# Two batches' logit extensions in one run of the tensor engine, with a longer x ring and loads tied to their own stores

## What is computed

```python
base_out = einsum('bti,oi->bto', x, W) + b
y = base_out + (x @ A[slot]) @ Bm[slot] * 2
logits = einsum('bsd,ed->bse', y, route_w)
topk_v, topk_idx = top_k(logits, 1)
route_weight = one_hot(topk_idx) * topk_v
h = einsum('bsd,erd->bser', y, A_ffn)
out = einsum('bser,eor->bso', route_weight[..., None] * h, Bw)
return x + out
```

## Time and profile before

| | |
|---|---|
| median of 3 runs | 289.58 us (289.46 to 289.77) |
| the profiled execution | 289.77 us, of which the span of the trace is 288.0 us |
| busy shares of the span | PE 98%, PEld 79%, DVE 70%, ACT 39%, POOL 4% |
| chain that ended last | PE 98% |
| one whole unit in the steady part | 26.8 us |
| one extension | 3.6 us from its first weight load to the next main product |

### The profile page before, as it was taken

The page is one execution under the profiler, slowest core; times in us unless marked ns, Lnnn a source line. Parts: engine busy times, 40 slices in busy tenths (PEclk is TensorE's granted clock), DMA queues, the critical chain, the costliest instruction groups (busy, mean ns, idle before and its releaser), DMA issues.

```text
span 288.0 us, 4401 instructions
## 1 busy us (share of the span) xinstructions
PE 282.7 (98%) x1700; PEld 226.2 (79%) x1700; DVE 202.4 (70%) x234; ACT 112.6 (39%) x166; POOL 12.5 (4%) x44
## 2 busy tenths in 40 slices
PE   8999999999999999999999999999999999999994
PEld 5999999996766885888588758857885888588993
DVE  0061200077698998799789969896998798699974
ACT  0001300196877532744373355427432642443300
POOL 6300030000000000000000000000000000000000
PEclk9999999999999999999999999999999999999998
DMA  7999999999980247759958993999499769536668
GB/s 250 406 408 395 402 416 411 373 415 424 418 373 6 93 200 272 312 178 404 386 203 296 409 364 137 380 366 381 140 378 391 263 220 420 238 127 256 272 236 277
DMA packets 19591, 88.52 MB, mean 307 GB/s; under 512 B 2410, under 2 KB 5106, under 8 KB 11762
## 3 DMA queue, kind: packets, MB, share of 16 engines
q1 hardware_dynamic: 16128, 84.87, 75.7%
q10 hardware_dynamic: 3442, 3.37, 3.5%
HBM read 54.60 MB, written 33.55 MB: 306 GB/s over the span
## 4 chain that ended last, share of the span: by engine, by line
PE 98%; DVE 0%; DVEq 0%; issue 0%
PE bank_out L661 16%; PE bank_h L738 11%; PE bank_h L739 10%; PE bank_h L740 10%; PE bank_out L699 10%; PE bank_out L701 10%; PE bank_out L700 10%; PE bank_e L723 10%; PE bank_h L668 1%; PE bank_r L661 1%; PE bank_h L661 1%; PE bank_e L661 1%; PE bank_l L675 1%; PE bank_l L661 1%; PE bank_l L749 1%; PE bank_r L758 1%
## 5 line engine op out<-in xcount | busy, mean ns | idle before, releaser
L405 ACT ACTIVATE x_hi<-x_ring 128x1024 fp32r<-128x1024 f32 (+1 forms) x72 | 69.0, 965 | 66.7 <-PE bank_h L740 65.9
L507 DVE TENSOR_TENSOR x_lo<-x_ring,x_hi 128x1024 fp32r<-128x1024 f32 (+1 forms) x72 | 78.9, 1102 | 11.9 <-ACT x_hi L405 10.1
L598 DVE TENSOR_TENSOR x_ring<-bank_out,x_ring 128x1024 f32<-128x1024 f32 (+1 forms) x71 | 78.4, 1106 | 1.7 <-PE bank_out L701 1.2
L738 PE MATMUL bank_h<-x_hi,m_hi 128*128 128x512 f32 (+1 forms) x144 | 54.1, 376 | 0.0
L739 PE MATMUL bank_h<-x_lo,m_hi 128*128 128x512 f32 (+1 forms) x144 | 53.3, 370 | 0.0
L740 PE MATMUL bank_h<-x_hi,m_lo 128*128 128x512 f32 (+1 forms) x144 | 53.2, 369 | 0.0
L699 PE MATMUL bank_out<-wh_hi,bw_hi 128*128 128x512 f32 (+1 forms) x143 | 53.1, 371 | 0.0
L701 PE MATMUL bank_out<-wh_hi,bw_lo 128*128 128x512 f32 (+1 forms) x143 | 53.0, 371 | 0.0
L700 PE MATMUL bank_out<-wh_lo,bw_hi 128*128 128x512 f32 (+1 forms) x143 | 53.0, 371 | 0.0
L661 PE MATMUL bank_out<-pt,w_ring 128*128 128x136 f32 x384 | 46.0, 281 | 0.0
L661 PEld LDWEIGHTS bank_out<-pt,w_ring 128*128 128x128 f32 x384 | 45.4, 192 | 0.7 <-DMA w_ring<-W 0.7
(11 more groups left out here) (79 smaller groups left out, 162.3 us busy)
## 6 DMA issues: line engine op xcount, KB each, us to landing
x_ring<-xT SPq DMA_DIRECT2D x32, 1024.0 KB, 7.6
outT<-x_ring SPq DMA_DIRECT2D x28, 1024.0 KB, 4.8
w_ring<-W SPq DMA_DIRECT2D x30, 512.0 KB, 10.3
outT<-x_ring SPq DMA_DIRECT2D x12, 256.0 KB, 2.9
w_ring<-W SPq DMA_DIRECT2D x4, 256.0 KB, 4.5
x_ring<-loraB ACTq DMA_DIRECT2D x8, 128.0 KB, 10.3
la<-loraA ACTq DMA_DIRECT2D x8, 128.0 KB, 13.1
x_ring<-BwT SPq DMA_DIRECT2D x1, 1024.0 KB, 11.1
```

Source lines behind the costliest of these rows:

```text
L405: act.activation(out, in_, ACT.Copy).then_inc(done, 1)
L507: dve.tensor_tensor(out, a, b, ALU.subtract).then_inc(done, 1)
L598: dve.tensor_tensor(x, out_banks(u, j), x, ALU.add).then_inc(v_out, 1)
L738: mm(h, m_hi[:, c, :], hi, start=(c == 0), stop=False)
```

## The change

Extensions are no longer made one at the head of each batch's unit. At unit 0 comes that of batch 0, at unit 1 those of batches 1 and 2, at unit 3 of 3 and 4, at unit 5 of 5 and 6, at unit 7 that of 7; units 2, 4 and 6 have none at their head. They need two banks, and the second is had by putting the count into the logits' bank. x of the second batch is now read one unit earlier, so the ring has 14 pieces, and the load behind store k is that of piece k + 14, into the slot that this very store empties. Two loads more go out in the first phase. A scratch region is made smaller so that the ring fits.

```diff
-    XRING = 12
+    XRING = 14
...
-        bank_e = psum("bank_e", [P, T])
+        bank_e = [psum(f"bank_e{i}", [P, T]) for i in range(2)]
         bank_h = psum("bank_h", [P, T])
-        bank_r = psum("bank_r", [P, T])
...
+        EXT_RUNS = {0: (0,), 1: (1, 2), 3: (3, 4), 5: (5, 6), 7: (7,)}
...
-            LAG = 2
+            LAG = 0
             LAST = NPIECES - NQ
             for k in range(LAST):
                 store(k)
                 if k >= LAG and k - LAG + XRING < NPIECES:
                     load_x(k - LAG + XRING)
...
-                dve.scalar_tensor_tensor(out=wh[:, :], in0=bank_r[:, :], scalar=0.0, in1=wh[:, :],
+                dve.scalar_tensor_tensor(out=wh[:, :], in0=bank_l[:, :], scalar=0.0, in1=wh[:, :],
...
+            def extension(b):
+                pe.wait_ge(g_ext, b + 1)
+                if b >= 2:
+                    pe.wait_ge(a_top, b - 1)
+                    pe.wait_ge(v_two, b - 1)
+                for r in range(C // NGROUPS):
+                    for g in range(NGROUPS):
+                        c = r * NGROUPS + g
+                        for k in x_pieces(b, c):
+                            if c == 0 or k not in x_pieces(b, c - 1):
+                                x_landed(pe, k)
...
+                        last = mm(bank_e[b % 2][g * GROUP:(g + 1) * GROUP, :], ext[b % 2][:, c, :], x_chunk(b, c),
+                                  start=(r == 0), stop=(r == C // NGROUPS - 1))
+                last.then_inc(t_ext, 1)
...
                 if leads(u):
-                    pe.wait_ge(g_ext, b + 1)
-                    if b >= 1:
-                        pe.wait_ge(a_top, b)
-                        pe.wait_ge(v_two, b)
...
+                    for n in EXT_RUNS.get(b, ()):
+                        extension(n)
...
                         if b >= 1:
-                            pe.wait_ge(a_log, b)
-                            pe.wait_ge(v_ahead, b)
+                            pe.wait_ge(v_w, b)
...
-                        if b >= 1:
-                            pe.wait_ge(v_w, b)
-                        mm(bank_r[:, :], beats[0:JUDGES, :], ahead[0:JUDGES, :], start=True, stop=True).then_inc(t_count, 1)
+                        mm(bank_l[:, :], beats[0:JUDGES, :], ahead[0:JUDGES, :], start=True, stop=True).then_inc(t_count, 1)
...
-    nc = bacc.Bacc("TRN2", target_bir_lowering=False, num_devices=1)
+    nc = bacc.Bacc("TRN2", target_bir_lowering=False, num_devices=1, dynamic_dma_scratch_size=1024)
```

More of the change, by code:

```diff
@@ L101, in adaln_ffn @@
         x_ring = sb("x_ring", [P, XRING, PIECE])
-        lb = x_ring[:, 8, :].rearrange("p (b c r) -> p b c r", b=NB, c=C)
-        bw_raw = x_ring[:, 9, :]
+        lb = x_ring[:, 12, :].rearrange("p (b c r) -> p b c r", b=NB, c=C)
+        bw_raw = x_ring[:, 13, :]
         lb_cols = x_ring[:, 11, :].rearrange("p (c b r) -> p c b r", b=NB, c=C)
-        EARLY = (8, 9, 11)
+        EARLY = (11, 12, 13)
         phase1 = ExitStack()
@@ L242, in w_banks @@
             if blk == 2:
-                return [(bank_e, 4, 1), (bank_h, 5, 1)]
+                return [(bank_e[0], 4, 1), (bank_h, 5, 1)]
             if blk == 3:
-                return [(bank_r, 6, 1), (bank_l, 7, 1)]
+                return [(bank_e[1], 6, 1), (bank_l, 7, 1)]
             return [(bank_out[blk % 2], 2 * blk, 2)]
@@ L438, in _ @@
                     act.wait_ge(t_pb, 1)
-                    copy(pb[:, E:XN], bank_r[0:1, 0:PN], a_bp)
-                    copy(pb[:, 0:E], bank_r[0:1, 0:E], a_bp)
+                    copy(pb[:, E:XN], bank_e[1][0:1, 0:PN], a_bp)
+                    copy(pb[:, 0:E], bank_e[1][0:1, 0:E], a_bp)
                     act.wait_ge(a_bp, 4)
@@ L469, in _ @@
                         act.wait_ge(v_two, b)
-                    act.activation(e_top[:, :], bank_e[2 * GROUP:4 * GROUP, :], ACT.Identity,
+                    act.activation(e_top[:, :], bank_e[b % 2][2 * GROUP:4 * GROUP, :], ACT.Identity,
                                    bias=e_bias[:, 0:1]).then_inc(a_top, 1)
@@ L554, in sum_two @@
                     dve.wait_ge(a_odd, b)
-                dve.tensor_tensor(e_two[:, :], bank_e[0:2 * GROUP, :], e_top[:, :], ALU.add).then_inc(v_two, 1)
+                dve.tensor_tensor(e_two[:, :], bank_e[b % 2][0:2 * GROUP, :], e_top[:, :], ALU.add).then_inc(v_two, 1)
             def sum_all(b):
@@ L680, in _ @@
             pe.wait_ge(g_const, CONSTS)
-            mm(bank_r[:, 0:PN], ones[:, :], pb_sum[(C - 1) % 2][:, :], start=True, stop=True).then_inc(t_pb, 1)
+            mm(bank_e[1][:, 0:PN], ones[:, :], pb_sum[(C - 1) % 2][:, :], start=True, stop=True).then_inc(t_pb, 1)
             for n in range(BP_AT, NWP):
@@ L707, in _ @@
             pe.wait_ge(a_beats, 3)
+            def extension(b):
[9 more added lines that the diff above has]
+                                x_landed(pe, k)
+                        if b == 0 and c % 2 == 0:
+                            pe.wait_ge(a_m, 3 * M_LOTS[c // 2])
+                        last = mm(bank_e[b % 2][g * GROUP:(g + 1) * GROUP, :], ext[b % 2][:, c, :], x_chunk(b, c),
+                                  start=(r == 0), stop=(r == C // NGROUPS - 1))
+                last.then_inc(t_ext, 1)
             for u, (b, t0, nt) in enumerate(UNITS):
                 if leads(u):
-                    pe.wait_ge(g_ext, b + 1)
-                    if b >= 1:
-                        pe.wait_ge(a_top, b)
-                        pe.wait_ge(v_two, b)
[L715 to L725, removed]
+                    for n in EXT_RUNS.get(b, ()):
+                        extension(n)
                 if u >= 1:
```

## The result

The changed kernel takes 323.9 us (median of six runs, 321.4 to 325.7) against 289.6 before (also six runs, 289.5 to 289.8), a ratio of 1.118 with a 95% interval of 1.113 to 1.124. I had said 295.5 and at most 298.8: the sign was right, the size was off by a factor of almost six.

What follows compares the result with a forecast made beforehand. PE, busy without a break in a steady unit, was taken to bound the kernel. The terms -1.0 + 1.7 + 3.3 + 2.0 = +6.0 us on 289.77 gave 295.8, or 295.5 us as median; range 292.0 to 298.8.

Steps and rivals of the forecast that it cites:

- The gain of the switches: Exits from extensions in the second phase: three switches fewer at 0.34 us each, 1.0 us less.
- First and second cost: Heads of units 2, 4, 6: PE waits for `weigh`, 1.7 us in all, and for the first addition, 3.3 us.
- Third cost: SP's queue: each load waits for its store's landing, so loads fall behind and PE waits in units 3 and 5, 2.0 us.
- p: Period of SP's loop per piece while stores are due: taken as 7.1 us, bounds 6.3 and 7.3.
- the harmless value: Period of SP's loop up to which PE loses nothing to late loads: 6.95 us.
- The clock: PE's clock: long gaps may halve it; no size given, only added to the rival of late loads.
- the rival of late loads: Loads much later, full 7.3 us period with second load delayed, or piece 11 late: above 298.5 us; chance 0.07.
- The fixed-cost estimate: SP's loop: 2.0 us plus two 1 MB transfers at 2.4 each, 6.8 us, no wait, 293.7 us whole; not chosen.
- Edits at nothing: Count in the logits' bank, two more first-phase loads, smaller scratch: claimed to cost nothing.

Runs made afterwards that it cites:

- the control: The kernel before, with only DVE's and ACT's order changed (additions moved ahead, chain of sums closed up): 289.4 us, ratio 0.9996.
- `LAG = 1`: The changed kernel with the load behind store k being that of piece k + 13, which waits for the store one piece back: 293.6 us, ratio 1.0125.

## Why the prediction was wrong, step by step

- **The gain of the switches** (1.0 us) is seen in the trace: five exits for eight. In time, once the waits are cleared, 0.65 us against the kernel before (0.3 to 1.0 by the interval) or 0.5 against the control.
- **First and second cost, the waits for DVE** (1.7 and 3.3 us): right in mechanism and place, and in size as a sum. With the loads cured the kernel takes 293.6 where these two costs and the gain gave 293.7 on the profiled execution, 293.5 on the median.
- **Third cost, loads behind their own stores: this is the step that failed**, in the size of one term. The mechanism and the pieces (19 and 27) were right, but "I take p = 7.1, between the row and the harmless value", with an upper end of 7.3, used a row in which the store is issued first. In the changed kernel the load is first, and p was 8.9. Put into the same sum, 100.7 + 3.9 + 13 x 8.9 + 4.8 = 225.1 against a need at 199.7: 25 us of waiting, where PE idled 22.4 for x and lost more at the lower clock. (The landing was mis-sized too, 4.8 us for 6.3 of that load.) The prediction said itself that the rows have the order the other way round, and then treated their value as the upper end. No row bounded the reversed pair at 7.3. The rows had no safe upper end either: a store alone was there with 3.9 us, a load alone was not. With the load alone at 4.7 to 5.0, measured afterwards, the plain sum of both is 8.6 to 8.9, and that is nearly the result.
- The same sum has p at thirteenfold: 0.1 us of doubt in p is 1.3 us of time beyond the threshold of 6.95. A range of 6.3 to 7.3 for p looked generous and was not; an estimate with such a lever needs an end that is measured.
- **The clock** had no term. It was named as an addition to the rival of late loads, with 0.07 for that rival, and it goes with the 6.6 us by which PE was busy longer than with `LAG = 1`. It came with the stops of 3.2 us and more that p = 8.9 makes; with `LAG = 1` PE's stops for DVE are 0.8 us at most and PEclk stays high. Stops of 1.0 and 1.1 us in two of the other kernels left it at 1.00 too; none between 1.1 and 3.2 us occurred.
- **The fixed-cost estimate** from the Trainium skill (DMA: Bandwidth & Descriptors, Anatomy of one DMA), 2.0 us and the bytes at 436 GB/s, gives 4.4 us for one transfer of 1 MB. The page fits this for DMAs issued from GpSimd, and these go out from SP. Alone, a load took 4.7 to 5.0 us and a store 3.9, so for one transfer it is within about 0.6 us all the same. It is the assumption laid on top, that the second of two adds only its bytes, which gave p = 6.8 and which no run shows for a load with a store behind it.
- **Edits at nothing** were at nothing: 1.0004 with the ring, banks, count and scratch changed and the rest as before.
- Shown by runs: that the line `LAG = 0` carries 30 us, that early reading does not, that the two waits for DVE carry the rest, that DVE's order removes them. Not settled: why a load begins slower than a store, which holds most of the 1.5 us between the two orders, and why the loop took 9.2 and 9.3 us in the two kernels with single extensions instead of 8.9. Each of these two, and the kernel with one transfer at a time, was run once; their distances of 20 to 40 us are far beyond the spread of the other kernels.

## What to carry to other kernels

- When an edit makes a queue wait for its own last transfer, work out the round trip and compare it with the pace at which items come due. If it is longer, lateness adds up with every item, and a small error in the round trip is multiplied by their number. Take the sum of the two lone transfers for it, not a pair measured in another order, and leave room above: that sum was 8.6 us here, and the loops took 8.9 to 9.3.
- Work that looks like a cost to PE (an extension at the head of each unit) may be the cover of another engine's chain. Before moving it, list what ends within it: here `weigh` 0.4 us too late for its absence and the first addition 1.2 us. Both could be cured by the order of the other engine, but only once the whole alternation was moved, not its first member alone, and the chain of sums closed up.
- A ring that is longer by two slots bought nothing while the rule for refilling it gave the two slots away; one more piece of lag kept them useful.

## What the runs showed of the hardware

- Two transfers of 1 MB on one queue, 0.4 us apart: store first, both landed after 7.4 us (kernel before) and 7.7 us (`LAG = 1`) as a median, 7.3 at least and 9.0 at most; load first, after 8.8 us in the pair shown, no sooner than one after the other (4.7 + 3.9 = 8.6 us).
- In the first 2 us from its issue a store alone moved 262 GB/s and a load alone 94; the pairs had 262 with the store first and 86 with the load first.
- In the kernels where PE's matmuls stopped for 3.2 to 8.0 us at a time the granted clock went to 0.50 and stayed there through the first matmuls afterwards (0.43 us apart against 0.23). With four such stops in two units PE was busy 6.6 us longer than in the same stream without them.
